# A recurrent first stage and its cross-attention, overlapped at the seam: the second stage's first unit between the first stage's last projection and its last output product, one subtraction moved to GpSimd, and the mean square read behind the scan

## The chip, the cores and the metric

The program runs on one core of a Trainium2 chip. The metric is the device time of one execution in microseconds (us). The core has five engines that each work through their own list of instructions in order: TensorE (PE; its weight loads are shown apart as PEld), VectorE (DVE), ScalarE (ACT), GpSimd (POOL) and SyncE (SP), which here only starts transfers. An engine waits for another by a counter (a semaphore).

## What is computed

The reference is a two-layer decoder on 16 sequences of 128 tokens with 256 channels, with a layer norm after each of its six sub-layers. The change touches the first two.

```
x = layernorm(x + hgrn(x))                 # stage A
x = layernorm(x + cross_attention(x, ctx)) # stage B
x = layernorm(x + top2_experts(x))         # stage C
...                                        # three more sub-layers
```

```
def hgrn(x):                       # stage A
    i, f, g = x @ Wi, x @ Wf, x @ Wg
    i = silu(i) * sigmoid(-f)
    a = sigmoid(f)
    o = scan over tokens: h = a * h + i
    o = o * rsqrt(mean(o*o) + eps) * gnorm * silu(g)
    return o @ Wo

def cross_attention(X, Z):         # stage B; X, Z are (channels, tokens) blocks
    q, k, v = Wq X + bq, Wk Z + bk, Wv Z + bv
    p = softmax(where(mask, k^T q, -inf) / sqrt(128))
    return v p
```

## The kernel before

The tokens are cut into NU = 8 units of two sequences (UB = 2, so 256 tokens a unit). Each stage is written out by hand, once for every engine, as a list of steps with lags: `pipelined(engine, NU, [(lag, step), ...])` calls, in turn s, each step of the list in its order for unit s - lag. Buffers are used by turns (`slot` is the unit's parity). Nothing is scheduled by a program: an engine runs what stands next in its list, and waits there.

Stage A, for a unit t:

- ACT `a_x_high` (L726) rounds the unit of X to its high part xp_hi; DVE `a_x_low` (L1101) subtracts that from X and writes the low part xp_lo (128x512). The three projections on PE, `a_proj` (L1606), are 36 matmuls that take products of high and low parts, and fill banks 0 to 5.
- ACT `a_gates` (L738 to L743) takes four sigmoids. DVE `a_scan` multiplies (L1121, L1126 from the banks; L1130, gb, from memory) and runs two scans (L1133), then multiplies the scan's result by the gate (L1140, og).
- ACT `a_square` (L753) squares the scan's result. PE `a_out` sums the squares with eight tiny matmuls (L1635) and makes the output product (L1640) in banks 7 and 6.
- DVE `a_msq` (L1147) reads the mean square; POOL `a_rms` (L610) takes its inverse root; DVE `a_sub` (L1157, y) adds the scaled product to X; the layer norm's statistics follow (L1077, L1081, and the variance L1083). POOL takes the root of the variance (L597) and makes the shift (L603, L606), and ACT `a_apply` (L758) writes the normalised rows back to X.

PE's `a_out` for a unit waits until the variance of the unit before is written, since bank 6 must have been read.

Stage B, for a unit: PE `b_proj` makes queries, keys and values (L1655, L1659, L1665, banks 0 to 2); ACT copies its context rows (`b_copy`, L772) and takes queries and values out of the banks (`b_evac`, L778 and L783), DVE the keys (`b_keys`, L1175); PE `b_scores` (L1676, L1677, banks 3 and 4); DVE takes the maximum (L1180), ACT the exponentials (`b_exp`, L792), DVE divides by the sum (L1184, L1189); PE transposes (`b_xpose`, L1688, banks 5 and 6) and makes the output (`b_out`, L1699, bank 7), and a layer norm follows (DVE L1196, L1077 to L1083, POOL L597, DVE L1090).

Between the two stages each engine first ends its list of stage A. DVE then waits for all rows of stage A to be normalised, makes the scaled bias and the mask (L1167, L1169), and only after these do ACT and PE begin stage B:

```
            pe.wait_ge(sem("B_consts"), 2)
            loaded(pe, "ld_b")
            pe.wait_ge(sem("ln_var"), LN["B"])
```

## Time and profile before

| | |
|---|---|
| median of three runs | 812.95 us (812.26 to 814.93) |
| the profiled execution | 808.24 us, of it 806.5 us from first to last instruction |
| PE busy | 704.8 us (87%) |
| DVE busy | 556.4 us (69%) |
| ACT busy | 469.1 us (58%) |
| POOL busy | 234.6 us (29%) |
| stage A, first projection to last variance | 7.7 to 84.7 us |
| stage B, first projection to last router product | 88.3 to 171.2 us |

The timeline view lists an engine's instructions in order of time; a row with xN merges N of them. The number in brackets at a row's end is how long the engine was idle before it, and what ended that wait. The view of windows gives, for a stretch of time, the busy time of each engine, then the clock that TensorE was granted (1.00 is the full 2.4 GHz, 0.50 is 1.2 GHz), then the share of the transfer engines and the rate in GB/s.

### The profile page before, as it was taken

How to read it: one execution, taken by the hardware profiler on the slowest of the kernel's cores; microseconds unless marked ns; L12 is line 12 of the kernel's file. 1: busy time of each engine (PE TensorE's matmuls, PEld its weight loads, DVE VectorE, ACT ScalarE, POOL GpSimd, SP SyncE). 2: the span in 40 equal slices, each digit the busy share in tenths (PEclk: the TensorE clock that was granted, in tenths of full speed). 3: DMA queues.
4: the chain of work that ended last, by engine and by line, in shares of the span. 5: the costliest groups of instructions: out<-in, count | busy, mean ns of one | idle time of the engine just before them, and what ended most of it. 6: DMA issues, size and time to landing. Idle time of an engine off the chain costs nothing.

```text
span 806.5 us, 17830 instructions
## 1 busy us (share of the span) xinstructions
PE 704.8 (87%) x5074; PEld 627.8 (78%) x5075; DVE 556.4 (69%) x1498; ACT 469.1 (58%) x1179; POOL 234.6 (29%) x399
## 2 busy tenths in 40 slices
PE   6887699958864988999999999999699989999972
PEld 5886477734432988999998999999599978888872
DVE  4786387757888446777786788887566765555376
ACT  4453466538782227777776788887345545555433
POOL 3122200033334600112121121111154515555544
PEclk9999699966695899999999999999699999999996
DMA  9940000000002586656667566652025433333162
GB/s 291 355 118 0 1 1 1 0 0 1 0 1 105 154 278 203 179 162 202 190 189 207 146 192 168 160 157 74 0 84 136 144 95 98 97 99 102 45 227 79
DMA packets 66486, 95.59 MB, mean 119 GB/s; under 512 B 11391, under 2 KB 52993, under 8 KB 66305
## 3 DMA queue, kind: packets, MB, share of 16 engines
q1 hardware_dynamic: 63024, 86.51, 36.3%
q0 software_dynamic: 3408, 8.43, 2.9%
q8 instruction: 26, 0.43, 0.2%
q14 instruction: 28, 0.22, 0.1%
HBM read 62.45 MB, written 33.36 MB: 119 GB/s over the span
## 4 chain that ended last, share of the span: by engine, by line
PE 58%; issue 16%; DVE 12%; DMA 4%; POOL 3%; ACT 3%; SPq 3%; DVEq 0%; POOLq 0%; ACTq 0%
PE bank L1875 13%; PE bank L1861 7%; PE bank L1951 6%; PE bank L2017 5%; PE bank L1850 4%; PE bank L1844 3%; PE bank L2041 3%; PE bank L1968 3%; PE bank L1606 3%; PE bank L1891 2%; PE bank L2005 2%; SPq L478 1%; DMA k_D<-stage_d 1%; DVE X L1090 1%; PE bank L1640 1%
## 5 line engine op out<-in xcount | busy, mean ns | idle before, releaser
L1875 PE MATMUL bank<-f_mem,late_mem 128*128 128x68 f32 (+3 forms) x1024 | 127.9, 268 | 0.0
L1875 PEld LDWEIGHTS bank<-f_mem,late_mem 128*128 128x128 f32 x1024 | 124.5, 192 | 0.7 <-issue 0.5
L597 POOL TENSOR_TENSOR rstd<-var,power 128x2 f32<-128x2 f32 (+1 forms) x64 | 41.7, 651 | 219.4 <-DVE var L1083 208.5
L1336 DVE TENSOR_REDUCE smax<-bank 128x4 f32<-128x512 f32 x128 | 88.2, 690 | 22.3 <-PE bank L1850 20.9
L915 ACT ACTIVATE late_mem<-bank 128x512 f32<-128x512 f32 x128 | 77.7, 607 | 21.6 <-PE bank L1861 19.3
L905 ACT ACTIVATE late_mem<-bank,smax 128x128 f32<-128x128 f32 x256 | 73.8, 384 | 11.4 <-DVE smax L1336 11.4
L1861 PE MATMUL bank<-ident,late_mem 128*128 128x128 f32 x512 | 77.3, 273 | 2.9 <-ACT late_mem L905 1.6
L1850 PE MATMUL bank<-kz,qs 128*128 128x256 f32 x256 | 75.1, 376 | 0.0
L1861 PEld LDWEIGHTS bank<-ident,late_mem 128*128 128x128 f32 x512 | 59.2, 141 | 3.6 <-ACT late_mem L905 2.0
L899 ACT ACTIVATE late_mem<-late_mem 128x512 f32<-128x512 f32 x64 | 41.0, 641 | 24.1 <-DVE late_mem L1343 23.3
L1850 PEld LDWEIGHTS bank<-kz,qs 128*128 128x128 f32 x256 | 48.7, 191 | 6.1 <-issue 0.3
L1951 PE MATMUL bank<-x_hi,w_hi 128*128 128x256 f32 x176 | 51.6, 293 | 1.0 <-DVE x_lo L1400 1.0
L1951 PE MATMUL bank<-x_lo,w_hi 128*128 128x256 f32 x176 | 50.8, 288 | 0.0
L1951 PE MATMUL bank<-x_hi,w_lo 128*128 128x256 f32 x176 | 50.7, 288 | 0.0
L1844 PE MATMUL bank<-causal,identb 128*128 128x512 bf16 x128 | 48.7, 381 | 1.2 <-DVE hidden_mem L1327 1.2
L1343 DVE TENSOR_TENSOR late_mem<-bank,smax 128x512 f32<-128x512 f32 x64 | 44.3, 692 | 6.9 <-DVE smax L1336 0.5
L686 POOL DMA_INDIRECT xg<-X,idx x32 | 33.6, 1049 | 42.7 <-DMA xg<-X,idx 21.2
L698 POOL DMA_INDIRECT yg<-attn_w,dest x39 | 38.8, 995 | 20.4 <-issue 12.0
L1968 PE MATMUL bank<-w_hi,hid_hi 128*128 128x256 f32 (+1 forms) x96 | 29.9, 311 | 13.8 <-DVE hid_lo L1417 13.7
L977 ACT ACTIVATE f_mem<-bank 128x256 f32<-128x256 f32 x40 | 15.3, 384 | 40.9 <-PE bank L1951 40.7
L1407 DVE TENSOR_TENSOR f_mem<-bank,f_mem 128x256 f32<-128x256 f32 x40 | 17.0, 424 | 30.0 <-ACT f_mem L977 29.7
L627 POOL TENSOR_TENSOR late_mem<-late_mem,f_mem 128x256 bf16<-128x256 bf16 x32 | 21.4, 669 | 52.1 <-DVE late_mem L1271 52.1
(285 smaller groups left out, 2069.9 us busy)
## 6 DMA issues: line engine op xcount, KB each, us to landing
qs<-q_D SPq DMA_DIRECT2D x64, 128.0 KB, 2.7
kz<-k_D SPq DMA_DIRECT2D x128, 64.0 KB, 2.6
qs<-q_E SPq DMA_DIRECT2D x64, 128.0 KB, 2.7
kz<-k_E SPq DMA_DIRECT2D x128, 64.0 KB, 2.5
xg<-f_mem SPq DMA_DIRECT2D x1, 5031.0 KB, 22.7
late_mem<-xg SPq DMA_DIRECT2D x39, 129.0 KB, 2.1
q_D<-stage_d SPq DMA_DIRECT2D x8, 512.0 KB, 2.9
k_D<-stage_d SPq DMA_DIRECT2D x8, 512.0 KB, 4.0
```

The lines of the kernel that those rows point to most:

```text
L597: gp.tensor_tensor(rstd[:, slot, 0:n], var[:, slot, 0:n], power[:, 0:n], ALU.pow).then_inc(sem("ln_rstd"), 1)
L899: sc.activation(sp[:, g, :, :], sp[:, g, :, :], ACT.Exp).then_inc(sem("core_exp"), 1)
L905: ins = sc.activation(sp[:, g, i, :], bank[g][:, i * P:(i + 1) * P], ACT.Exp, bias=smax[:, g, i:i + 1])
L915: sc.activation(spt[:, g, :, :], bank[4 + g % 2][:, :], ACT.Copy).then_inc(sem("core_pts"), 1)
L1336: ve.tensor_reduce(smax[:, g, :], v, axis=AX.X, op=ALU.max, negate=g not in SUBS).then_inc(sem("core_max"), 1)
L1343: ve.tensor_tensor(sp[:, g, :, :], v, smax[:, g, :].unsqueeze(2).to_broadcast([P, HG, P]), ALU.subtract).then_inc(sem("core_sub"), 1)
L1844: mm(bank[g][:, :], identb[:, :], causal[:, :].unsqueeze(1).to_broadcast([P, HG, P]), start=True, stop=False)
L1850: ins = mm(bank[g][:, i * D:(i + 1) * D], qs[slot][:, a_ * P:(a_ + 1) * P], kz[:, slot, :, a_ * P:(a_ + 1) * P], start=False, stop=(i == 1))
L1861: ins = nc.tensor.transpose(bank[4 + g % 2][:, i * P:(i + 1) * P], sp[:, g, i, :], ident[:, :])
L1875: ins = mm(bank[6][:, h * (DH + 1):to * (DH + 1)], spt[:, g, i, :], vf[:, slot, h:to, :].rearrange("p h d -> p (h d)"), start=True, stop=True)
L1951: ins = mm(bank[r][:, m * UT:(m + 1) * UT], w[:, lo:lo + P], x[:, t % 2, k, :], start=(n == 1), stop=(n == 3 * KC))
L1968: ins = mm(halves(6 + t % 2)[:, j, :], h[lanes, r, cols], v[lanes, w], start=(f == n == j == 0), stop=(f == NF - 1 and n == 2 and j == UB ...
```

## The change

Four things are changed; all other code is the same.

1. Low part of X: `a_x_low` moves from DVE's list to POOL's, at the head of each turn, for units 1 to 7. Unit 0's stays on DVE. On POOL the steps `a_rms`, root and shift have lag 2 instead of 1, which leaves their order among themselves as it was.
2. Mean square: DVE's `a_scan` is split. The multiplication og is now its own step `a_gated`, and `a_msq` stands between the scans and it.
3. PE's `a_out` waits for the two reads of bank 6 by `a_sub` (`ln_stats`) instead of for the variance.
4. Seam: `b_proj` and `b_scores` of unit 0 stand on PE between `a_proj` of unit 7 (and `a_out` of unit 6) and `a_out` of unit 7. ACT's and DVE's steps for that unit are put into the last turns of stage A: the bias and mask at the end of DVE's turn 7, the rest in turns 8 and 9. The exponentials of unit 0 stand on ACT between the `a_apply` of units 6 and 7, and their division on DVE between mean square and `a_sub` of unit 7. ACT loads one table with both exponential and logarithm ahead of them, and the load that stood ahead of stage C is gone. PE's transposes of unit 0 wait for the last variance of stage A.

```
+            def a_x_low(t, slot):
+                pool.wait_ge(sem("A_xh"), t + 1)
+                gp.tensor_tensor(xp_lo[:, slot, :, :], tokens(XT, t), xp_hi[:, slot, :, :], ALU.subtract
+                                 ).then_inc(sem("A_xl"), 1)
-            pipelined(pool, NU, [(1, a_rms), (1, inverse_root("A")), (1, a_shift)])
+            pipelined(pool, NU, [(0, but_first(a_x_low)), (2, a_rms), (2, inverse_root("A")), (2, a_shift)])
...
-            pipelined(act, NU, [(0, a_x_next), (1, a_gates), (1, a_square), (3, a_apply)])
...
-            pipelined(act, NU, [(0, b_copy), (1, b_evac), (2, b_pt), (4, c_xt), (1, b_exp)])
+            def exp_table():
+                sc.preload_act_table_set("natural_log_exp_and_others")
+            pipelined(act, NU, [(0, a_x_next), (1, only_at(NU - 1, (b_copy, (0, 0)))), (1, a_gates),
+                                (1, only_at(NU - 1, (b_evac, (0, 0)))), (1, a_square),
+                                (1, only_at(NU - 1, (b_evac_v, (0, 0)))), (3, but_last(a_apply)),
+                                (1, only_at(NU - 1, (b_copy, (1, 1)), (exp_table, ())))])
+            b_exp(0, 0)
+            a_apply(NU - 1, (NU - 1) % 2)
+            pipelined(act, NU, [(0, lambda t, slot: None if isinstance(t, int) and t < 2 else b_copy(t, slot)),
+                                (1, but_first(b_evac)), (1, but_first(b_evac_v)), (2, b_pt), (4, c_xt),
+                                (1, but_first(b_exp))])
...
-            pipelined(dve, NU, [(0, a_x_next), (1, a_scan), (2, a_msq), (2, stats)])
-            dve.wait_ge(sem("ln_x"), LN["B"])
...
-            pipelined(dve, NU, [(0, b_keys), (2, apply), (0, b_max), (2, c_copy), (3, c_scores), (1, stats)])
+            pipelined(dve, NU, [(1, a_scan), (2, a_msq), (2, only_at(NU - 1, (b_norm, (0, 0)))), (1, a_gated),
+                                (1, only_at(NU - 1, (b_keys, (0, 0)))), (2, a_stats),
+                                (1, only_at(NU - 1, (b_max, (0, 0)))), (1, only_at(NU - 2, (b_consts, ())))])
+            pipelined(dve, NU, [(0, but_first(b_keys)), (2, apply), (0, but_first(b_max)), (0, but_first(b_norm)),
+                                (2, c_copy), (3, c_scores), (1, stats)])
...
                 if not (isinstance(t, int) and t < 1):
-                    pe.wait_ge(sem("ln_var"), t)
+                    pe.wait_ge(sem("ln_stats"), 3 * UB * t - 2 * UB)
...
-            pipelined(pe, NU, [(0, a_proj), (1, a_out)])
-            pe.wait_ge(sem("B_consts"), 2)
-            pe.wait_ge(sem("ln_var"), LN["B"])
...
+            pipelined(pe, NU, [(0, a_proj), (1, only_at(NU - 1, (b_proj, (0, 0)), (b_scores, (0, 0)))), (1, a_out)])
+            pipelined(pe, NU, [(0, but_first(b_proj)), (1, b_xpose), (3, c_xpose), (0, but_first(b_scores)), (3, c_router),
+                               (1, b_out)])
```

How the lists stand now. First DVE, one turn of stage A, before (late turns stand outside the loop, in the loop's order; up_mem holds the gates and the scan, bank the projections; "waits" names the semaphores waited for):

```order
L1101 TENSOR_TENSOR xp_lo<-XT_mem,xp_hi 128x512 [waits A_xh]
L1121 TENSOR_TENSOR up_mem<-bank,up_mem 128x512 [waits A_gates]
L1124 MEMSET up_mem 128x4
L1126 TENSOR_TENSOR up_mem<-bank,up_mem 128x512
L1130 TENSOR_TENSOR up_mem<-up_mem 128x512 [waits A_si,A_hsq]
L1133 SCALAR_TENSOR_TENSOR up_mem<-up_mem 128x256 [waits A_own]
L1133 SCALAR_TENSOR_TENSOR up_mem<-up_mem 128x256
L1140 TENSOR_TENSOR up_mem<-up_mem 128x512 [waits A_h,A_si,A_o]
L1147 TENSOR_SCALAR msq<-bank 128x2 [waits A_o]
L1157 SCALAR_TENSOR_TENSOR y<-bank,rms,X 128x256 [waits ln_x,A_rms]
```

With the change:

```order
L1146 TENSOR_TENSOR up_mem<-bank,up_mem 128x512 [waits A_gates]
L1149 MEMSET up_mem 128x4
L1151 TENSOR_TENSOR up_mem<-bank,up_mem 128x512
L1155 TENSOR_TENSOR up_mem<-up_mem 128x512 [waits A_si,A_hsq]
L1158 SCALAR_TENSOR_TENSOR up_mem<-up_mem 128x256 [waits A_own]
L1158 SCALAR_TENSOR_TENSOR up_mem<-up_mem 128x256
L1174 TENSOR_SCALAR msq<-bank 128x2 [waits A_o]
L1167 TENSOR_TENSOR up_mem<-up_mem 128x512 [waits A_h,A_si,A_o]
L1184 SCALAR_TENSOR_TENSOR y<-bank,rms,X 128x256 [waits ln_x,A_rms]
```

The subtraction is gone from the head of DVE's turn, and the mean square (now L1174) stands ahead of og (now L1167). On POOL the subtraction heads the turn:

```order
L632 ISA [waits A_xh]
L632 TENSOR_TENSOR xp_lo<-XT_mem,xp_hi 128x512
L626 REGISTER_ALU
L627 TENSOR_TENSOR rms<-msq,power 128x2 [waits A_msq]
L614 TENSOR_TENSOR rstd<-var,power 128x2 [waits ln_var]
L620 TENSOR_TENSOR nmean<-mv,minus 128x2
L623 TENSOR_TENSOR nbias<-nmean,rstd 128x2 [waits ln_rstd,A_minus]
```

It stands behind the shift of the turn before, that is behind the variance of the unit three before. PE at the seam, before (behind unit 7's projection and unit 6's output product):

```order
L1635 MATMUL bank<-ones,up_mem 128x1 [waits ln_var,A_hsq]
L1635 MATMUL bank<-ones,up_mem 128x1 x3
L1640 MATMUL bank<-late_mem,up_mem 128x256 [waits A_og]
L1640 MATMUL bank<-late_mem,up_mem 128x256 x3
L1655 MATMUL bank<-X,hidden_mem 128x512 [waits ln_var,ld_b,ln_x,B_consts,consts]
L1659 MATMUL bank<-f_mem,hidden_mem 128x512 [waits B_xs]
```

and with the change:

```order
L1684 MATMUL bank<-X,hidden_mem 128x512 [waits A_gates,A_si,ld_b,ln_x]
L1688 MATMUL bank<-f_mem,hidden_mem 128x512 [waits B_xs]
L1694 MATMUL bank<-hidden_mem,f_mem 128x128 x4
L1709 MATMUL bank<-maskb,identb 128x256 [waits B_consts,consts,A_si,B_ks,B_qs]
L1710 MATMUL bank<-late_mem 128x256
```

```order
L1668 MATMUL bank<-ones,up_mem 128x1 [waits ln_stats,A_hsq]
L1668 MATMUL bank<-ones,up_mem 128x1 x3
L1673 MATMUL bank<-late_mem,up_mem 128x256 [waits A_og]
L1673 MATMUL bank<-late_mem,up_mem 128x256 x3
L1684 MATMUL bank<-X,hidden_mem 128x512 [waits B_qs,ln_x]
L1688 MATMUL bank<-f_mem,hidden_mem 128x512 [waits B_ks,B_xs]
L1694 MATMUL bank<-hidden_mem,f_mem 128x128 [waits B_vs]
L1694 MATMUL bank<-hidden_mem,f_mem 128x128 x3
L1724 MATMUL bank<-ident,late_mem 128x128 [waits B_p,ln_var,A_si]
```

Unit 0's projection and scores (L1684 to L1710) are ahead of unit 7's output product (L1668, L1673) now; unit 1's projection follows it at once, and the first wait for the end of stage A is at the transposes (L1724). ACT in the same place, with the change:

```order
L781 ACTIVATE X<-y,nbias,rstd 128x256 [waits A_shift]
L781 ACTIVATE X<-y,nbias,rstd 128x256
L814 ACTIVATE late_mem,psum_row<-bank,nmax 128x256 [waits B_max]
L814 ACTIVATE late_mem,psum_row<-bank,nmax 128x256
L814 ACTIVATE late_mem,psum_row<-bank,nmax 128x256 [waits B_max]
L814 ACTIVATE late_mem,psum_row<-bank,nmax 128x256
L781 ACTIVATE X<-y,nbias,rstd 128x256 [waits A_shift]
L781 ACTIVATE X<-y,nbias,rstd 128x256
L790 ACTIVATE f_mem<-ctx_mem 128x512 [waits B_proj]
L798 ACTIVATE late_mem<-bank,bqs 128x512 [waits B_q]
```

The queries of unit 1 leave their bank (L798) only behind unit 7's `a_apply` (the second L781 pair), which waits for the last shift of stage A.

## Rows read from the trace of the kernel before

**Rows 1.** Windows: stretch, busy us (instructions) by engine, PE clock, DMA share, GB/s
```profile
28.50:32.70 4.20, 4.16 (x16) 3.62 (x17) 3.98 (x8) 0.30 (x1) 1.02 (x3) 0.59 1.08 369
88.20:93.80 5.60, 5.54 (x14) 3.44 (x15) 0.75 (x1) 1.89 (x4) 0.85 (x1) 0.50 0.01 3
95.90:164.00 68.10, 65.06 (x381) 51.45 (x379) 51.54 (x161) 43.00 (x114) 5.46 (x8) 1.00 0.00 1
```
**Rows 2.** Timeline of DVE, stage A: start us, us, what [idle before]
```profile
36.19 0.17 DVE L1083 TENSOR_SCALAR var<-mv 128x2 f32<-128x2 f32 x1
...
54.13 0.68 DVE L1121 TENSOR_TENSOR up_mem<-bank,up_mem 128x512 f32<-128x512 f32 x1
...
56.06 1.27 DVE L1133 TENSOR_TENSOR_SCAN up_mem<-up_mem 128x256 f32<-128x256 f32 x2
57.46 0.69 DVE L1140 TENSOR_TENSOR up_mem<-up_mem 128x512 f32<-128x512 f32 x1
...
59.15 0.87 DVE L1157 SCALAR_TENSOR_TENSOR y<-bank,rms,X 128x256 f32<-128x256 f32 x2 [0.93 <-POOL rms L610]
...
61.13 0.17 DVE L1083 TENSOR_SCALAR var<-mv 128x2 f32<-128x2 f32 x1
61.32 0.69 DVE L1101 TENSOR_TENSOR xp_lo<-XT_mem,xp_hi 128x512 fp32r<-128x512 f32 x1
61.93 0.68 DVE L1121 TENSOR_TENSOR up_mem<-bank,up_mem 128x512 f32<-128x512 f32 x1
```
**Rows 3.** Timeline of PE: a turn of stage A, the seam, unit 1 of stage B
```profile
32.72 0.47 PE L1606 MATMUL bank<-xp_hi,wa_hi 128*128 128x256 f32 x1
...
37.22 0.95 PE L1635 MATMUL bank<-ones,up_mem 128*128 128x1 f32 x8
38.03 1.97 PE L1640 MATMUL bank<-late_mem,up_mem 128*128 128x256 f32 x8
...
76.48 1.46 PE L1635 MATMUL bank<-ones,up_mem 128*128 128x1 f32 x8 [4.50 <-DVE var L1083]
...
88.26 2.04 PE L1655 MATMUL bank<-X,hidden_mem 128*128 128x512 f32 x2 [6.70 <-DVE maskb L1169]
...
99.47 0.27 PE L1676 MATMUL bank<-maskb,identb 128*128 128x256 bf16 x1
...
101.64 1.89 PE L1699 MATMUL bank<-late_mem 128*128 128x256 f32 x8
```
**Rows 4.** Timeline of POOL: stage A, and a subtraction of the same shape
```profile
58.30 0.69 POOL L610 TENSOR_TENSOR rms<-msq,power 128x2 f32<-128x2 f32 x1 [3.10 <-DVE msq L1147]
61.38 1.18 POOL L597 TENSOR_TENSOR rstd<-var,power 128x2 f32<-128x2 f32 x1 [2.38 <-DVE var L1083]
...
62.79 0.20 POOL L606 TENSOR_TENSOR nbias<-nmean,rstd 128x2 f32<-128x2 f32 x1
...
164.71 1.26 POOL L636 TENSOR_TENSOR wd_lo<-attn_w,wd_hi 128x512 fp32r<-128x512 f32 x1
```
**Rows 5.** Timeline of POOL, near the end
```profile
790.75 1.21 POOL L708 TENSOR_TENSOR X<-X,late_mem 128x512 f32<-128x512 f32 x1
```
**Rows 6.** Timeline of DVE, the same stretch
```profile
790.83 1.68 DVE L1567 TENSOR_TENSOR ctx_mem<-ctx_mem,late_mem 128x512 f32<-128x512 f32 x1
```
**Rows 7.** Timeline of ACT, the seam and unit 0 and 1 of stage B
```profile
85.95 1.09 ACT L758 ACTIVATE X<-y,nbias,rstd 128x256 f32<-128x256 f32 x2 [7.29 <-POOL nbias L606]
...
94.37 1.28 ACT L792 ACT_TABLE_LOAD   x1
95.75 0.47 ACT L792 ACTIVATE late_mem<-bank,nmax 128x256 f32<-128x256 f32 x1
...
97.75 0.62 ACT L772 ACTIVATE f_mem<-ctx_mem 128x512 f32<-128x512 f32 x1
```
**Rows 8.** Timeline of DVE, the mask, and half of the division of unit 0
```profile
87.15 1.01 DVE L1169 TENSOR_SCALAR maskb<-mask 128x512 bf16<-128x512 uint8 x1
...
98.09 0.62 DVE L1189 TENSOR_SCALAR late_mem<-late_mem,rrow 128x256 f32<-128x256 f32 x2
```

More of the change, by code:

```diff
@@ L120, in pipelined_pair, with but_first, other, only_at @@
         turn(s)
+def but_first(step):
+    def other(t, slot):
+        if not (isinstance(t, int) and t == 0):
+            step(t, slot)
+    return other
+def only_at(turn, *steps):
+    def other(t, slot):
+        if isinstance(t, int) and t == turn:
+            for step, args in steps:
+                step(*args)
+    return other
 RING = 3
@@ L809, in c_xt, with but_last, other @@
                 sc.activation(tokens(XTB, t), halves(2), ACT.Copy).then_inc(sem("C_xt"), 1)
-            pipelined(act, NU, [(0, b_copy), (1, b_evac), (2, b_pt), (4, c_xt), (1, b_exp)])
+            def but_last(step):
+                def other(t, slot):
+                    if not (isinstance(t, int) and t == NU - 1):
+                        step(t, slot)
+                return other
+            def exp_table():
[9 more added lines that the diff above has]
+                                (1, but_first(b_exp))])
             def route_exp():
@@ L852, in _ @@
             route_exp()
-            def but_first(step):
-                def other(t, slot):
-                    if not (isinstance(t, int) and t == 0):
-                        step(t, slot)
-                return other
             def c_round(t, slot):
@@ L1107, in _ @@
                 if k == 0:
-                    a_x_low(0, 0)
-            def a_x_next(t, slot):
-                if not (isinstance(t, int) and t < 1):
-                    a_x_low(t, slot)
+                    dve.wait_ge(sem("A_xh"), 1)
+                    ve.tensor_tensor(xp_lo[:, 0, :, :], tokens(XT, 0), xp_hi[:, 0, :, :], ALU.subtract
+                                     ).then_inc(sem("A_wl"), 1)
             loaded(dve, "ld_a2")
@@ L1135, in a_scan, with a_gated @@
                 ins.then_inc(sem("A_h"), 1)
+            def a_gated(t, slot):
                 if not (isinstance(t, int) and t < 2):
@@ L1194, in b_sub @@
                 dve.wait_ge(sem("B_o"), t + 1)
+                if isinstance(t, int) and t < 1:
+                    dve.wait_ge(sem("ln_x"), LN["B"])
                 for j in range(UB):
@@ L1612, in a_proj @@
             def a_proj(t, slot):
-                pe.wait_ge(sem("A_xl"), t + 1)
+                if not (isinstance(t, int) and t < 1):
+                    pe.wait_ge(sem("A_xl"), t)
                 if not (isinstance(t, int) and t < 2):
@@ L1654, in b_proj @@
                     pe.wait_ge(sem("B_qs"), t)
+                else:
+                    loaded(pe, "ld_b")
+                    pe.wait_ge(sem("A_gates"), 4 * NU - 2)
+                    pe.wait_ge(sem("A_si"), 2 * NU - 3)
                 mm(halves(0), xq[:, :], xrows(t), start=True, stop=True).then_inc(sem("B_q"), 1)
@@ L1670, in b_scores @@
                 pe.wait_ge(sem("B_ks"), t + 1)
+                if isinstance(t, int) and t < 1:
+                    pe.wait_ge(sem("consts"), CONSTS)
+                    pe.wait_ge(sem("B_consts"), 2)
+                    pe.wait_ge(sem("A_si"), 2 * NU - 1)
                 for j in range(UB):
@@ L1681, in b_xpose @@
             def b_xpose(t, slot):
+                if isinstance(t, int) and t < 1:
+                    pe.wait_ge(sem("A_si"), 2 * NU)
+                    pe.wait_ge(sem("ln_var"), LN["B"])
                 for j in range(UB):
```

27 lines of the change are left out of this document (12 added, 15 removed).

## The prediction
> **What bounds the kernel now.** I read the slices of the page first: TensorE is 87% busy over the span, with two thin places early on, and the change touches only the first 165 us. So I asked three things. What sets the turn of stage A? What lies empty at the seam? And is stage B, behind it, bound by PE, so that a start earlier by so much ends earlier by as much?
>
> The turn of stage A: from unit 5's first multiplication at 54.13 to unit 6's at 61.93 is 7.80 us [rows 2]. DVE does nothing else but work through its list, and stands idle 0.93 us once, ahead of y, for POOL's root. PE's turn at full clock takes 4.50 us of projection (32.72 to 37.22) and 2.78 us of sums and output product, whose end overlaps the next projection: 7.3 us at most, I take 7.0 [rows 3]. So DVE bounds stage A, and PE is 0.8 us behind.
>
> The seam: PE waits 4.50 us for the variance ahead of unit 7's sums, and 6.70 us for the mask ahead of stage B [rows 3], and after the second wait it runs at a granted clock of 0.50 (1.2 GHz) for 5.6 us [rows 1].
>
> Stage B: from 95.9 to 164.0 us PE is busy 65.1 of 68.1 us at clock 1.00 [rows 1], while DVE and ACT are busy 52 and 43. PE bounds it from unit 1 on. I measure the gain at one point therefore: the start of unit 1's scores, 99.47 us before [rows 3]. What is earlier there is earlier at the end.
>
> **The turn of stage A.** Edit 1 takes 0.61 us (61.32 to 61.93) [rows 2] from DVE's turn and edit 2 lays og's 0.61 over POOL's root. If nothing else happened, DVE's turn would be 7.80 - 0.61 - 0.6 = 6.6 us and PE would bound.
>
> Two rows say that it will not be so. DVE's multiplication of two SBUF operands took 1.68 us at 790.83, against 0.69 for one of that shape at 57.46 [rows 6, 2]; POOL's addition of the same shape had begun 0.08 us earlier and lasted till 791.96 [rows 5], and DVE ended 0.55 behind it. The other way round, POOL's root at 61.38, begun 0.06 behind DVE's subtraction, took 1.18 instead of 0.69 and ended 0.55 behind that [rows 4, 2]. So these pairs do not overlap: the later waits out the earlier. The Trainium skill (SBUF — State Buffer, Who interferes with whom) says this of every Vector instruction with two SBUF inputs beside a GpSimd one that reads SBUF, which speaks against both moves of stage A; by that rule the trace agrees, and it leaves y free, whose one operand is a bank.
>
> Now I follow one turn from V, the end of a variance. POOL's root starts 0.08 later and takes 0.69 (nothing blocks it now), the shift ends 0.43 behind it (62.56 to 62.99) [rows 4]: V + 1.2. The subtraction starts at V + 1.3 and takes 1.26, the duration of the one of that shape and type at 164.71 [rows 4]: V + 2.56. DVE wants gb (two SBUF inputs) about 1.2 us behind the start of its turn, so inside this stretch; it ends at V + 3.11. Scans to the start of og: 1.40 (56.06 to 57.46) [rows 2], so V + 4.55. og ends at V + 5.24. The root of the mean square starts about 0.05 behind og (the mean square itself ends as the scans do), is blocked, and ends at V + 5.79; y starts 0.16 later (58.99 to 59.15), and the next variance ends 2.15 behind that (59.15 to 61.30) [rows 2]: 8.10 us a turn, against 7.80.
>
> PE does not shorten that: unit 1's variance ended at 36.36 [rows 2]; with mean square earlier and the first collisions I put it at 36.0. Four turns give 68.4, and the bias and mask on DVE, now between turns 7 and 8, 1.1 (1.01 for the mask [rows 8]): unit 7's first multiplication starts at 69.5. Stage A gains nothing. The bounds of a turn are 7.3 (no collision; PE's limit) and 8.5 (the subtraction itself blocked, at the 1.68 us of a blocked instruction [rows 6]).
>
> **The seam.** From 69.5, in order:
> - og ends 4.0 later (54.13 to 58.15) [rows 2], the keys behind it 0.7 (a 128x512 instruction, [rows 2]): 74.3. PE has made unit 0's projection meanwhile; ACT has copied and evacuated in its idle time.
> - Scores of unit 0: 2.2 (99.47 to 101.64) [rows 3]: 76.5. Sums and output product of unit 7: 2.8 [rows 3]: 79.3. This is the removed wait of 4.50, now filled.
> - On ACT, the table load (1.28) [rows 7] is over before unit 6's shift comes: y of unit 6 starts at 74.3, variance 76.4, shift 77.6. Apply takes 1.0 [rows 7], the four exponentials 2.0 (95.75 to 97.75) [rows 7]: 80.6. **This is a new wait**: the division of unit 0 stands on DVE ahead of y of unit 7, and ends 0.8 behind the exponentials [rows 8], 81.4, though POOL's root of unit 7 was ready at about 80.2.
> - y and variance of unit 7, 2.15: 83.6. PE's transposes of unit 0 can start. The shift is there at 84.8.
> - On ACT apply of unit 7 (1.0), the copy for unit 2 and the queries of unit 1 (two 128x512 instructions of 0.6) [rows 7] follow one another: 87.0. Scores of unit 1 start at 87.1.
>
> The Trainium skill (ScalarE: Activation LUTs, What ACT_TABLE_LOAD costs) gives about 2.66 us for a switch with its drain; here 94.37 to 95.75 [rows 7] shows 1.38 to the next instruction, so the row decides. By the page's figure apply of unit 6 would start 0.5 later and the sum would be 0.5 higher.
>
> 99.47 - 87.1 = **12.4 us earlier**. Against this: PE has work for only 1 us (the transposes) between unit 1's projection, which ends at about 81.9, and 87.1. Twice in these stages the clock was down with PE busy: 28.5 to 32.7 at 0.59, a loss of 4.2 x 0.41 = 1.7 us, and 88.2 to 93.8 at 0.50, a loss of 2.8 us [rows 1]. Unit 1's scores and unit 0's output product should lie in such a stretch now, behind the point at which I measure. Nothing is the lower bound; the second row has a long gap in front, as here, so I take **2.8**. The second table load that goes was not waited for, and stage C starts as before. Edit 3 (the wait for the reads) only starts products that then wait for a projection: nothing.
>
> Sum: 12.4 - 2.8 = 9.6 us less. On the profiled execution's 808.24 that is 798.6; it lies 4.7 below the median of the runs, 812.95, from which I take the same 9.6: **803.4 us**.
>
> **Rivals.**
> - The collisions cost less: POOL's root may come before og and then be free of it (8.1 - 0.55 = 7.55 a turn), or the subtraction finds DVE busy with instructions that do not collide (PE's 7.3). Four turns give 2.2 to 3.2 more, in the middle 800.7. For it: 0.05 us is a thin margin. Against it: two rows show full blocking.
> - The clock stays up: PE stands still 1.7 us, works 1.0, and stands still 2.5, no single gap as long as the 4.50 and 6.70 of before. Then the 2.8 us are not lost: 800.6; with the case above 797.9.
> - The collisions cost more, or the in-order waits of the two interleaved stages add up: 8.5 a turn is 1.6, and each of ACT and DVE could be a step late, another 2: 807.0.
> - No difference: stage A's list on DVE turns out so much slower that it eats the seam; that takes turns of over 10 us.
> - **Slower:** in stage A PE now stands still about 8.1 - 7.0 = 1.1 us a turn or more, before 0.8. If that makes its clock fall and stay down, a turn takes twice PE's 7.0, 14 instead of 8.1 us. Two such turns take 11.8 us and more than the gain; all five make 29.5, so 812.95 - 9.6 + 29.5 = 832.8. It decides where a gap outlasts what the clock forgives, which lies above the 0.8 of before and at or below the 4.50 of the seam. Against it: a turn longer by 0.3 us changes little.
>
> **How the numbers follow.** The forecast gets 0.50; more gain (fewer collisions, the clock kept, or both) 0.32; dearer collisions 0.10; no difference 0.04; slower 0.04. The predicted time is that of the likeliest, 803.4. The range takes in both gains nearly whole and the dearer case: 798.0 to 808.0. A measurement of this kernel tells 0.3% (2.4 us) from no change. Faster by that: 0.50 + 0.32 + 0.10 = 0.92, within it 0.04, slower 0.04.
>
> **What would show it.** In DVE's timeline gb (L1155) at 1.2 to 1.5 us instead of 0.68, and POOL's L627 at about 1.2 instead of 0.69, say that the pairs collide; turns of 8.1. PE's unit 7 sums directly behind scores with no idle; DVE's y of unit 7 behind the division of unit 0 and not behind POOL; PE's scores of unit 1 released by ACT's queries, at 87, in a window at clock 0.5 to 0.6. From there to the end every distance as before. I am wrong if the gain does not stand at the scores of unit 1, if stage A's turn leaves 7.3 to 8.5, or if PE is idle inside stage B from unit 2 on.

## The result, and the profile after

| | before | with the change |
|---|---|---|
| median | 813.25 us (812.26 to 814.93) | 802.84 us, three executions (798.12 to 802.98) |
| ratio, 95% interval | | 0.9851 (0.9804 to 0.9898) |
| profiled execution, and its span | 808.24 us, 806.5 us | 802.98 us, 801.2 us |
| PE / DVE / ACT / POOL busy | 704.8 / 556.4 / 469.1 / 234.6 us | 706.2 / 556.6 / 466.9 / 244.9 us |

The forecast was 803.4 us. The changed kernel was run twice more, as the control of the experiments; the ratio was 0.9865 both times. The medians fell by 10.4, 11.9 and 12.0 us. The ratio is not the quotient of the two medians (that is 0.987 here and 0.985 in both controls), so the two readings of a total differ by up to 0.2%. A fourth execution of the changed kernel took 1689.29 us and is left out here and in the ratio; with it the median would be 802.91 us.

First a turn of stage A, the one that [rows 2] show of before. The timeline of DVE, changed kernel; columns as there:

```profile
53.53 0.69 DVE L1146 TENSOR_TENSOR up_mem<-bank,up_mem 128x512 f32<-128x512 f32 x1 [0.55 <-ACT up_mem L766]
...
54.75 1.24 DVE L1155 TENSOR_TENSOR up_mem<-up_mem 128x512 f32<-128x512 f32 x1
56.02 1.27 DVE L1158 TENSOR_TENSOR_SCAN up_mem<-up_mem 128x256 f32<-128x256 f32 x2
57.21 0.14 DVE L1174 TENSOR_SCALAR msq<-bank 128x2 f32<-128x2 f32 x1
57.33 0.69 DVE L1167 TENSOR_TENSOR up_mem<-up_mem 128x512 f32<-128x512 f32 x1
58.72 0.88 DVE L1184 SCALAR_TENSOR_TENSOR y<-bank,rms,X 128x256 f32<-128x256 f32 x2 [0.70 <-POOL rms L627]
...
60.70 0.17 DVE L1115 TENSOR_SCALAR var<-mv 128x2 f32<-128x2 f32 x1
61.43 0.69 DVE L1146 TENSOR_TENSOR up_mem<-bank,up_mem 128x512 f32<-128x512 f32 x1 [0.56 <-ACT up_mem L766]
```

The timeline of POOL in the same turn:

```profile
53.06 0.69 POOL L614 TENSOR_TENSOR rstd<-var,power 128x2 f32<-128x2 f32 x1 [2.40 <-DVE var L1115]
...
54.17 1.27 POOL L632 TENSOR_TENSOR xp_lo<-XT_mem,xp_hi 128x512 fp32r<-128x512 f32 x1
57.42 1.14 POOL L627 TENSOR_TENSOR rms<-msq,power 128x2 f32<-128x2 f32 x1 [1.99 <-DVE msq L1174]
```

The turn is 7.90 us (53.53 to 61.43), against 7.80. Both collisions are there. gb (L1155) began inside POOL's subtraction, took 1.24 us instead of 0.68, and ended 0.55 behind it (54.17 + 1.27 = 55.44; 54.75 + 1.24 = 55.99). The root of the mean square began 0.09 behind og, took 1.14 and ended 0.54 behind it, where before it took 0.69 [rows 4]. And DVE now waits 0.55 us at the head of its turn for ACT's gates, since PE waits for the same subtraction: in PE's timeline the idle of 0.71 below. The work that left DVE came back as waits. From variance to variance, units 1 to 5, the turns are 7.89, 8.26, 7.89 and 7.86 us; before they were 8.86, 8.26, 7.82 and 7.68.

So one turn, unit 2's, did get shorter, and for another reason. PE ahead of unit 1's sums, in the kernel before and in the changed one:

```profile
28.54 1.32 PE L1635 MATMUL bank<-ones,up_mem 128*128 128x1 f32 x8 [2.54 <-DVE var L1083]
```

```profile
27.55 1.05 PE L1668 MATMUL bank<-ones,up_mem 128*128 128x1 f32 x8 [0.81 <-DVE y L1184]
```

Before, PE waited 2.54 us for the variance, and the granted clock behind that wait was 0.59 from 28.5 to 32.7 [rows 1]. With edit 3 it waits 0.81 us, for y's read of the bank, and the clock stays at 1.00. Of the 13 profiles of kernels with edit 3, the controls and the experiments included, 12 have unit 2's turn at 7.1 to 7.9 us; the exception is told below. No run has edit 3 alone, so that it is the cause is argued and not shown.

Then the seam, the timeline of PE:

```profile
55.67 0.38 PE L1638 MATMUL bank<-xp_hi,wa_hi 128*128 128x256 f32 x1 [0.71 <-POOL xp_lo L632]
...
74.10 0.27 PE L1709 MATMUL bank<-maskb,identb 128*128 128x256 bf16 x1 [0.77 <-issue]
...
76.27 0.95 PE L1668 MATMUL bank<-ones,up_mem 128*128 128x1 f32 x8
...
83.23 1.06 PE L1724 MATMUL bank<-ident,late_mem 128*128 128x128 f32 x8 [1.57 <-issue]
86.60 0.39 PE L1709 MATMUL bank<-maskb,identb 128*128 128x256 bf16 x1 [2.30 <-ACT late_mem L798]
...
90.84 2.34 PE L1735 MATMUL bank<-late_mem 128*128 128x256 f32 x8
93.01 1.02 PE L1684 MATMUL bank<-X,hidden_mem 128*128 128x512 f32 x2
```

The waits of 4.50 and 6.70 us [rows 3] are gone. Unit 7's sums (76.27) follow unit 0's scores directly. What is left are 0.77, 1.57 and 2.30 us. The first two have no releaser in the view ("issue"): the first ends 0.11 us behind the keys of unit 0 (DVE's L1198, 73.25 to 73.99), the second 0.10 behind the variance of unit 7 (83.13), for which the transposes wait. The last is for the queries of unit 1. These start at 86.60, against 99.47 [rows 3]. The timelines of DVE and ACT say why they were not there sooner:

```profile
68.70 0.42 DVE L1192 TENSOR_SCALAR maskb<-mask 128x512 bf16<-128x512 uint8 x1
69.31 0.69 DVE L1146 TENSOR_TENSOR up_mem<-bank,up_mem 128x512 f32<-128x512 f32 x1 [0.19 <-ACT up_mem L766]
...
80.98 0.87 DVE L1184 SCALAR_TENSOR_TENSOR y<-bank,rms,X 128x256 f32<-128x256 f32 x2
...
82.96 0.17 DVE L1115 TENSOR_SCALAR var<-mv 128x2 f32<-128x2 f32 x1
```

```profile
75.49 1.28 ACT L840 ACT_TABLE_LOAD   x1
77.31 1.09 ACT L781 ACTIVATE X<-y,nbias,rstd 128x256 f32<-128x256 f32 x2 [0.54 <-POOL nbias L623]
...
84.36 1.09 ACT L781 ACTIVATE X<-y,nbias,rstd 128x256 f32<-128x256 f32 x2 [4.15 <-POOL nbias L623]
85.36 0.61 ACT L790 ACTIVATE f_mem<-ctx_mem 128x512 f32<-128x512 f32 x1
85.88 0.67 ACT L798 ACTIVATE late_mem<-bank,bqs 128x512 f32<-128x512 f32 x1
```

ACT stands 4.15 us ahead of unit 7's apply, and the queries of unit 1 (L798), whose bank PE had filled by about 80, are queued behind it. Last, the clock, by windows (columns as in [rows 1]):

```profile
84.00:85.00 1.00, 0.29 (x3) 0.05 (x1) 0.00 (x0) 0.64 (x2) 0.92 (x3) 0.95 0.00 0
85.00:86.00 1.00, 0.00 (x0) 0.00 (x0) 0.00 (x0) 1.00 (x3) 1.00 (x2) 0.50 0.00 0
...
91.00:92.00 1.00, 1.00 (x5) 0.80 (x4) 0.88 (x3) 0.19 (x1) 0.00 (x0) 0.63 0.00 0
```

The granted clock is 0.50 from 85 to about 91.5 (before it was 0.50 from 77 to 94). The scores of unit 1 and the output of unit 0 took 6.41 us together (86.60 to 93.01), against 3.90 before (99.47 to 103.37).

### The profile page after: what moved, and what is told of

It reads as the page before. It is cut to its first block, busy times and chain, and to the rows that moved or that the text cites. A ratio compares the mean times of both kernels' runs of the same rounds, so it can differ in the third digit from the quotient of the medians.

```text
span 801.2 us, 17829 instructions
## 1 busy us (share of the span) xinstructions
PE 706.2 (88%) x5074; PEld 628.8 (78%) x5075; DVE 556.6 (69%) x1491; ACT 466.9 (58%) x1178; POOL 244.9 (31%) x406
## 4 chain that ended last, share of the span: by engine, by line
PE 56%; issue 15%; DVE 14%; ACT 5%; DMA 3%; POOL 3%; SPq 2%; DVEq 0%; POOLq 0%; ACTq 0%
PE bank L1913 13%; PE bank L1899 7%; PE bank L2055 5%; PE bank L1989 5%; PE bank L1638 4%; PE bank L1888 4%; PE bank L1882 3%; PE bank L2079 3%; PE bank L2006 3%; PE bank L1929 2%; PE bank L2043 2%; SPq L495 1%; POOL rstd L614 1%; DVE X L1122 1%; PE bank L1805 1%
## 5 line engine op out<-in xcount | busy, mean ns | idle before, releaser
L721 POOL DMA_INDIRECT yg<-attn_w,dest x39 | 38.8, 994 | 20.7 <-issue 12.6
L2006 PE MATMUL bank<-w_hi,hid_hi 128*128 128x256 f32 (+1 forms) x96 | 30.4, 317 | 14.6 <-DVE hid_lo L1449 14.3
L1638 PE MATMUL bank<-xp_hi,wa_hi 128*128 128x256 f32 x96 | 29.0, 302 | 12.4 <-DVE xp_lo L1135 8.1
```

What stands on the lines that cost most here:

```text
L1638: ins = mm(out, a_, b_, start=(n == 1), stop=(n == 3 * len(terms)))
L2006: ins = mm(halves(6 + t % 2)[:, j, :], h[lanes, r, cols], v[lanes, w], start=(f == n == j == 0), stop=(f == NF - 1 and n == 2 and j == UB ...
```

## How far one profile carries

The changed kernel's profile is 10.8 us ahead of the one before at unit 0's variance in stage B (95.57 against 106.33), and only 5.3 us at the end: it lost 5.5 us in code that, but for a table load, the edit does not touch. The two controls tell what that is.

> The changed kernel once more, with nothing edited, to have it on the same chip as the three runs below and to see how far executions of one and the same program lie apart. Expected: a median within 1.5 us of 802.9, a ratio to the kernel before of 0.987 (0.984 to 0.990), unit 7's first multiplication within 0.3 us of 69.3 and the scores of unit 1 within 0.3 us of 86.6. If single executions of one program spread by up to 5 us, as the 798.1 beside 802.8 and 803.0 suggests, the offset between the two traces behind the seam cannot be read from one profile of each; if they don't, the 4 to 5 us that the traces lose between stage C and the end are an effect of the change.

Measured: 801.3 us (795.72 to 802.56), ratio 0.9865 (0.9842 to 0.9889). Unit 7's first multiplication was at 68.63 and the scores of unit 1 at 85.92, both 0.7 us earlier than expected.

> The change as it is, on the same chip as the three others of this group. Expected: ratio 0.984 to 0.989 as in its first two measurements, unit 7's first multiplication within 0.8 us of 69.3, seven steady turns as before; its profile once more shows where executions of one program differ: the start (loads, up to 0.8 us), the low clock of the seam (0 to 2.5 us), and low-clock stretches between 160 and 460 us.

Measured: 800.28 us (798.01 to 803.75), ratio 0.9865 (0.9827 to 0.9903). Here the two places are 67.94 (outside the expected 0.8 us) and 85.23. Both differences were there at the start. DVE's second multiplication of unit 0, in the kernel before and in the profile above:

```profile
15.43 0.68 DVE L1126 TENSOR_TENSOR up_mem<-bank,up_mem 128x512 f32<-128x512 f32 x1
```

```profile
16.18 0.68 DVE L1151 TENSOR_TENSOR up_mem<-bank,up_mem 128x512 f32<-128x512 f32 x1
```

In the controls it is at 15.45 and 14.82. Counted from it, the scores of unit 1 start at 84.04 before and at 70.42, 70.47 and 70.41 in the three profiles of the change: 13.6 us earlier each time.

What lies behind the seam is less steady. Two variances in the timeline of DVE, the first control:

```profile
128.03 0.17 DVE L1115 TENSOR_SCALAR var<-mv 128x2 f32<-128x2 f32 x1
...
315.34 0.15 DVE L1115 TENSOR_SCALAR var<-mv 128x1 f32<-128x1 f32 x1
```

and the second:

```profile
127.51 0.17 DVE L1115 TENSOR_SCALAR var<-mv 128x2 f32<-128x2 f32 x1
...
318.80 0.15 DVE L1115 TENSOR_SCALAR var<-mv 128x1 f32<-128x1 f32 x1
```

The same instructions of the same program took 187.3 us in one execution and 191.3 in the other. Of the 4.0 us, 2.7 arise before 245 us, in a stretch with many low-clock pieces: from 150 to 260 us the granted clock changes between 0.50 and 1.00 several times, and where it does so differs from profile to profile. The first control is 12.6 us ahead of before at stage B's first variance and 12.5 at the last one of all; for the second control it is 12.8 and 10.2, for the profile shown above 10.8 and 5.3. So from here on a place is read in the profile, and a total from the ratio and the medians alone.

## The experiments

**The seam alone.** Stage A's edits 1 and 2 are undone; edit 3 stays. The part on DVE (the subtraction's step goes back from POOL's list to DVE's too):

```
-            pipelined(dve, NU, [(1, a_scan), (2, a_msq), (2, only_at(NU - 1, (b_norm, (0, 0)))), (1, a_gated),
+            pipelined(dve, NU, [(0, but_first(a_x_low)), (1, a_scan), (1, a_gated), (2, a_msq), (2, only_at(NU - 1, (b_norm, (0, 0)))),
```

> The seam alone: stage A's two edits are undone (the low parts back on VectorE at the head of its turn, the mean square behind the gated product), the moved first unit of stage B stays. Theory (the seam carries the gain, stage A's edits are a wash): steady turns of 7.80 us, unit 7's first multiplication at 69.3, the gated product of VectorE's unit 7 ahead of the mean square of unit 6, which puts y of unit 6 and the keys of unit 0 about 0.7 us later, scores of unit 1 at 86.6 to 87.3; median 0 to 1 us above the control. Rival (stage A's edits carry part of the gain): unit 7's first multiplication at 71 or later and a median 2 us or more above the control.

Measured: 800.1 us, ratio 0.9855 (0.9831 to 0.9879); turns of 7.83 and 7.80 us, scores of unit 1 at 86.59. The theory holds: with the seam and edit 3 there, edits 1 and 2 bring nothing. Unit 2's turn is 7.81 us here too, against 8.86 before, so that shorter turn is not theirs.

**Stage A's edits alone**, in the kernel before. Edit 3 is among them:

```
-            pipelined(dve, NU, [(0, a_x_next), (1, a_scan), (2, a_msq), (2, stats)])
+            pipelined(dve, NU, [(1, a_scan), (2, a_msq), (1, a_gated), (2, stats)])
-            pipelined(pool, NU, [(1, a_rms), (1, inverse_root("A")), (1, a_shift)])
+            pipelined(pool, NU, [(0, but_first(a_x_low)), (2, a_rms), (2, inverse_root("A")), (2, a_shift)])
...
-                    pe.wait_ge(sem("ln_var"), t)
+                    pe.wait_ge(sem("ln_stats"), 3 * UB * t - 2 * UB)
```

> The kernel before with stage A's two edits alone (low parts on GpSimd, mean square ahead of the gated product, the output product waiting for bn_stats in place of the variance), the seam as before. Theory: the collisions take back what the edits give; steady turns of 7.9 us, unit 7's first multiplication at 69.3, stage B's start as before; 812 to 814, that is within 1 us of the kernel before. Rival: the edits gain by themselves and the seam needs less; turns of 7.4 and 809 or lower.

Measured: 809.54 us, ratio 0.9946 (0.9924 to 0.9968). Both were wrong: a gain of about 4 us (3.6 by the medians, 4.4 by the ratio), and yet turns of 7.9. The timeline of PE, this kernel:

```profile
73.42 1.84 PE L1648 MATMUL bank<-ones,up_mem 128*128 128x1 f32 x8 [3.70 <-DVE y L1169]
...
85.59 2.04 PE L1668 MATMUL bank<-X,hidden_mem 128*128 128x512 f32 x2 [6.70 <-DVE maskb L1181]
```

The steady turns gain nothing, but the last two do. From unit 5's variance to unit 7's it is 14.3 us here (67.55 to 81.87) and 15.7 before (68.81 to 84.55), as the last turn is a bare chain, in which an earlier mean square counts, and as PE, by edit 3, no longer waits for the variance (3.70 against 4.50 us [rows 3]). Another 1.0 us is unit 2's turn, 8.86 us before and 7.90 here, with the granted clock at 1.00 where before had 0.59. With the seam, unit 0's projection and scores fill that wait of PE, and the last two turns are as long with edits 1 and 2 as without (14.4 us in either profile): what they bring there alone, the seam has already taken.

**One edit undone each.** The low parts back on VectorE, at the head of its turn:

> The changed kernel with one part undone: the low parts of X back on VectorE at the head of its turn, the mean square still ahead of the gated product. Theory (it is the shared port of VectorE and GpSimd that takes the gain of stage A: gb took 1.2 to 1.6 us beside the subtraction, 0.68 without): gb at 0.68, the gate product of unit s+1 behind a subtraction of 0.69, turns of 7.4 us; unit 7's first multiplication at 66.6 to 67.5 and a median 2 to 3 us below the control. Rival (VectorE's own work bounds the turn, so moving 0.7 us back costs it): turns of 8.3 or more and a median 2 us above the control. If the root of the mean square still takes 1.2 us here, it is the gated product beside it, not the subtraction, that slows it.

Measured: 794.45 us, ratio 0.9796 (0.9761 to 0.9831), outside the interval of the control: a gain over the change as it is. The timeline of DVE, this kernel:

```profile
50.76 0.69 DVE L1140 TENSOR_TENSOR xp_lo<-XT_mem,xp_hi 128x512 fp32r<-128x512 f32 x1
...
52.58 0.68 DVE L1155 TENSOR_TENSOR up_mem<-up_mem 128x512 f32<-128x512 f32 x1
...
58.09 0.17 DVE L1109 TENSOR_SCALAR var<-mv 128x2 f32<-128x2 f32 x1
```

gb is 0.68 again and the turn 7.54 us (variances at 50.55 and 58.09). The root of the mean square still took 1.25, so it is og that blocks that one. What the profile shows in place is 2.0 us at stage B's first variance (91.71 against 93.73 in the first control), of which 0.5 was there at unit 0's first multiplication. The forecast was a median 2 to 3 us lower; the medians differ by 6.9. The rest is not shown in any place, and by the section above executions of one program differ by as much.

The mean square back behind og, the low parts left on GpSimd:

> The fourth corner of stage A's two edits, with the seam kept: low parts on GpSimd, mean square back behind the gated product. Measured so far are both undone (800.1 us, turns of 7.8), low parts on VectorE with the mean square ahead (794.5, turns of 7.54), and both as changed (801.3, turns of 7.9). Theory (the two edits are independent terms: mean square ahead saves about 0.3 us a turn, the subtraction on GpSimd costs about 0.35): turns of 8.1 to 8.3 us and 803 to 805. Rival (the mean square ahead only helps where the low parts are on VectorE, since its root then runs beside the gated product and the two cancel): turns of 7.9 and 801.

Measured: 805.11 us, ratio 0.989 (0.9855 to 0.9926), turns of 8.2. A turn of the four combinations: 7.80 (both undone), 7.54 (mean square ahead), 8.2 (low parts on GpSimd), 7.9 (both). The edits are two independent terms, -0.3 and +0.4 us. This is also the one profile with edit 3 in which the clock fell in stage A: 0.50 from 29.5 to 36, behind a wait of PE of 1.10 us, and unit 2's turn took 9.07; the change as it is waited 0.81 and 1.65 us there and kept the clock. So 0.9 us of this profile (9.07 against 8.2) is not the collision's price. Here gb met the subtraction earlier in its course and waited longer, and again ended 0.55 behind it (POOL's row first):

```profile
55.68 1.26 POOL L632 TENSOR_TENSOR xp_lo<-XT_mem,xp_hi 128x512 fp32r<-128x512 f32 x1
```

```profile
55.96 1.53 DVE L1155 TENSOR_TENSOR up_mem<-up_mem 128x512 f32<-128x512 f32 x1
```

**The low parts at another place of GpSimd's turn**, between the two roots:

```
-            pipelined(pool, NU, [(0, but_first(a_x_low)), (2, a_rms), (2, inverse_root("A")), (2, a_shift)])
+            pipelined(pool, NU, [(3, a_rms), (0, but_first(a_x_low)), (3, inverse_root("A")), (3, a_shift)])
```

> The changed kernel with the low parts still on GpSimd, but one place later in its turn: between the root of the mean square and the root of the variance, so that they run beside y and bn_stats of VectorE in place of gb and the scans. Theory (what costs in stage A is that the subtraction meets gb and the scans on the shared port): gb back at 0.68 us, the two scans at 1.27, turns of 7.4 to 7.6 us, and a ratio to the kernel before of 0.980 like the run with the low parts on VectorE (794.5 us there). Rival (the subtraction costs the turn wherever it meets VectorE, or the root behind it comes late): turns of 7.9 or more, ratio 0.986 or above.

Measured: 796.4 us, ratio 0.9797 (0.9765 to 0.983), turns of 7.35 us. Timelines of POOL and of DVE, this kernel:

```profile
41.25 1.26 POOL L632 TENSOR_TENSOR xp_lo<-XT_mem,xp_hi 128x512 fp32r<-128x512 f32 x1 [1.08 <-ACT xp_hi L749]
```

```profile
41.24 0.75 DVE L1109 BATCH_NORM_STATS2 st<-y 128x6 f32<-128x256 f32 x2
...
44.26 0.68 DVE L1155 TENSOR_TENSOR up_mem<-up_mem 128x512 f32<-128x512 f32 x1
```

The same subtraction, on the same engine, now lies beside bn_stats (0.75, as everywhere) and neither takes longer; PE has no wait over 0.2 us between 28 and 69 us any more. The root of the mean square still takes 1.14 beside og. This settles the cause in stage A: not the load of an engine, but which instruction of the other lies beside it. The Trainium skill (SBUF — State Buffer, Who interferes with whom) has it that a Vector instruction with at most one SBUF input, outside the modes that use two ports, does not contend with GpSimd; the trace agrees, with 0.75 for bn_stats beside the subtraction and without it.

**The queries first** on ScalarE:

```
-            a_apply(NU - 1, (NU - 1) % 2)
...
-                                (1, but_first(b_evac)), (1, but_first(b_evac_v)), (2, b_pt), (4, c_xt),
+                                (1, but_first(b_evac)), (1, but_first(b_evac_v)), (1, only_at(1, (a_apply, (NU - 1, (NU - 1) % 2)))), (2, b_pt), (4, c_xt),
```

> The changed kernel with one move on ScalarE: the application of stage A's last unit stands behind the evacuation of unit 1's queries and values, not ahead of it. Theory (the scores of unit 1 started late, 2.3 us of TensorE idle, because ScalarE stood 4.15 us waiting for unit 7's nbias with the queries behind it): that idle goes down to the wait for the keys, some 0.3 us; scores of unit 1 begin 4.4 us behind the end of the values' product instead of 4.9 - that is 84.2 instead of 86.6 on the clock of the control's shape, and the shorter pause may save some of the low clock too: ratio 0.9865 less 0.003 to 0.006. Rival (the scores wait for something else of the same time, keys or the freed bank, or the saved time is given back at unit 0's output): ratio unchanged and another releaser on the idle.

Measured: 797.32 us, ratio 0.9788 (0.9743 to 0.9833). The timeline of PE, this kernel:

```profile
83.03 1.06 PE L1723 MATMUL bank<-ident,late_mem 128*128 128x128 f32 x8 [1.57 <-issue]
83.93 0.27 PE L1708 MATMUL bank<-maskb,identb 128*128 128x256 bf16 x1
...
87.83 1.02 PE L1683 MATMUL bank<-X,hidden_mem 128*128 128x512 f32 x2
```

The scores of unit 1 stand directly behind the transposes, and they and the output of unit 0 take 3.90 us (83.93 to 87.83), with the granted clock at 1.00 in every window from 66 to 102 us. The wait of 2.30 was the queries' place in a list, and without it the clock did not fall, though the wait of 1.57 is still there. All seven profiles that keep the 2.30 us wait (the change, its controls and four experiments) have a stretch of 0.50 behind it. At stage B's first variance this profile is 2.9 us ahead of the first control's, although its stage A ran 0.5 us later. The ratio is lower than the 0.9805 to 0.9835 that was expected; its interval takes in nearly all of that.

**Filling the pauses** with matmuls whose results nobody reads (n1 = 12 and n2 = 16, then 12 and 20):

```
+            def keep_warm(sem_name, count, b, n):
+                pe.wait_ge(sem(sem_name), count)
+                for k in range(n):
+                    mm(halves(b)[:, k & 1, :], identb[:, :], maskb[:, k & 1, :], start=True, stop=True)
-            pipelined(pe, NU, [(0, but_first(b_proj)), (1, b_xpose), (3, c_xpose), (0, but_first(b_scores)), (3, c_router),
+            pipelined(pe, NU, [(0, but_first(b_proj)), (0, only_at(1, (keep_warm, ("A_si", 2 * NU, 5, n1)))), (1, b_xpose),
+                               (0, only_at(1, (keep_warm, ("A_msq", NU, 7, n2)))),
+                               (3, c_xpose), (0, but_first(b_scores)), (3, c_router),
```

> The changed kernel with 12 matmuls (128x256, bf16, results never read) on TensorE in the pause ahead of the transposes of unit 0, and 16 in the pause ahead of the scores of unit 1. Theory (the low clock of 85 to 91 us follows the pauses of 1.6 and 2.3 us): the granted clock stays at 1.00 through the scores of unit 1 and the output of unit 0, which then take 2.17 and 1.73 us in place of 4.24 and 2.17 in the slowest profile, and the whole gains 1 to 2.5 us: ratio 0.984 to 0.986. Rival (the clock falls for what came before, the waits of stage A's end and the light load of the seam, or falls a little later instead): the low stretch stays or moves behind, and nothing is gained.

Measured: 803.94 us, ratio 0.9882 (0.9847 to 0.9917). The timeline of PE, with 12 and 16:

```profile
80.61 1.47 PE L1765 MATMUL bank<-maskb,identb 128*128 128x256 bf16 x12
82.34 1.06 PE L1724 MATMUL bank<-ident,late_mem 128*128 128x128 f32 x8 [0.26 <-issue]
83.24 1.91 PE L1765 MATMUL bank<-maskb,identb 128*128 128x256 bf16 x16
85.72 0.28 PE L1709 MATMUL bank<-maskb,identb 128*128 128x256 bf16 x1 [0.56 <-ACT late_mem L798]
```

The clock stayed at 1.00, the scores and the output took 3.91 us (85.72 to 89.63), and the profile was ahead of the control at stage B. So the low clock does follow the pauses. But the expected gain did not come: the median is 2.6 us above the control's, and the intervals of the two ratios overlap. The place where this profile loses is the loop of the routed experts 600 us later: from the last variance ahead of it to the first behind it, 214.2 us against 206.7 in the first control. The window of 680 to 730 us in the first control, and under it in this kernel:

```profile
680.00:730.00 50.00, 47.18 (x320) 42.04 (x319) 27.06 (x100) 25.96 (x80) 27.59 (x61) 1.00 0.34 102
```

```profile
680.00:730.00 50.00, 46.38 (x303) 40.16 (x304) 25.49 (x96) 24.93 (x76) 26.80 (x59) 1.00 0.32 96
```

Every other kernel did 319 or 320 matmuls there, at the same clock. The fill with 32 instead of 28 was made to ask whether the loop's place in PE's program matters:

> The fill of the pauses once more, with 12 and 20 dummy matmuls in place of 12 and 16. In the run with 28 the granted clock stayed at 1.00 through the seam, as its theory had it, and yet the time rose by 2.6 us: TensorE did 303 matmuls between 680 and 730 us where every other kernel did 319 or 320, in the routed experts' loop, which the edit does not touch. Theory (it is where the loop lies in TensorE's program: 28 matmuls with their weight loads are 56 more instructions ahead of it, and 32 make it 64, a round number): 319 or 320 matmuls in 50 us again and a ratio 0.984 to 0.986. Rival (dummy matmuls as such, or the data they read, slow the loop; or 64 is no better a shift than 56): 303 to 310 matmuls, ratio 0.988 or above.

Measured: 797.72 us, ratio 0.9813 (0.9772 to 0.9855), and in the window:

```profile
680.00:730.00 50.00, 47.33 (x320) 42.14 (x319) 26.95 (x100) 26.22 (x80) 27.73 (x60) 1.00 0.34 100
```

320 again, with more dummy matmuls than before, and 207.9 us for the stretch of the loop. So it is not the dummies as such. That it goes with how many instructions stand ahead of the loop fits both fills, but rests on one profile of each and is not shown. Why 56 more should cost 5% of the matmuls in 50 us and 64 nothing is open. The Trainium skill (Runtime: NRT & Kernel Launch, Instruction fetch mechanics) names a stall where the target of a taken branch is not in the two pages that are held and must be fetched first; the bytes on the instruction queues are 0.43 and 0.22 MB in both fills and in the control, so no run here shows an additional fetch.

**Both corrections together**, the queries first and the low parts on VectorE, and then with the low parts between GpSimd's two roots:

> Two corrections together: the low parts back on VectorE (mean square still ahead of the gated product), and stage A's last application behind the queries and values of unit 1 on ScalarE. Theory (they are terms of separate places, stage A's turn and the seam, and add up: 0.9796 and 0.9788 by themselves against 0.9865 for the change as it is): turns of 7.54 us, unit 7's first multiplication at 66.9, scores of unit 1 at 81.6 with TensorE at the full clock through the seam, ratio 0.972 to 0.977, 791 to 794. Rival (both mostly changed the share of executions that keep the full clock later on, and that is to be had once): ratio 0.978 or above.

Measured: 794.24 us (793.67 to 795.08), ratio 0.9783 (0.9748 to 0.9817): the rival's ratio. In place the terms do add up: stage B's first variance is at 88.07, 5.7 us ahead of the first control. But the profile then loses 4.7 us of its lead over the one before by the last variance (18.3 to 13.6), part of it right behind 140 us: the granted clock is 0.70 from 140 to 144, and the step between two variances there (139.63 to 145.99) takes 6.4 us, against 5.2 before. The total by itself cannot say whether this is worth more than either part.

> The same with the low parts on GpSimd between the two roots in place of VectorE. Theory: turns of 7.35 us as in the run that had this alone, unit 7's first multiplication at 65.8, scores of unit 1 at 80.5, and a ratio of 0.970 to 0.976, 1 us below the run with VectorE; below it if that 1 us is all. Rival: no better than the move of the low parts alone, 0.980.

Measured: 790.88 us (788.92 to 792.5), ratio 0.9744 (0.9708 to 0.9779), as forecast, with turns of 7.35 and the scores of unit 1 at 80.22. It is 3.4 us below the run with VectorE by the medians, where 1 was forecast, but the intervals of the two overlap. Its interval lies below that of the change as it is in all three measurements: 21 us under the kernel before, where the change is 10 to 12 under it.

## Why the prediction was right

The total was within a microsecond, and inside the range in the controls too. The nearness is in part luck: the forecast gain was 9.6 us, and the three measurements have 10.4, 11.9 and 12.0. The mechanism is the one forecast; what was short is named below. By its own steps:

- **The point of measurement.** "Scores of unit 1 at 87.1", 12.4 us earlier: 86.60, 12.9 earlier, or 13.6 when both are counted from unit 0. Each step of the chain was 0.3 to 0.5 early and in its order: end of the exponentials 80.2 (forecast 80.6), end of the division 81.07 (81.4), variance of unit 7 83.1 (83.6), its shift 84.3 (84.8). The new wait it named, y of unit 7 behind the division of unit 0, is there: 80.98, with no idle for POOL ahead of it.
- **The turn.** Forecast 8.10 for each of four, measured 7.89, 8.26, 7.89 and 7.86: 31.9 us instead of 32.4. Mechanism right, both collisions with the sizes told; the sum had 0.1 too much ahead of the subtraction (it began 1.19 behind the variance's end, not 1.3) and 0.1 between gb and og.
- **Unit 7's first multiplication**, forecast 69.5, was at 69.31 by errors that cancel. Unit 1's variance ended at 36.83 instead of 36.0, of which 0.75 was there at unit 0's multiplications; in the first control, which starts as before did, it ended at 36.11. The subtraction met the scans there, which took 2.22 instead of 1.27 us, and the turn was 8.06 against 7.96 before. The mask took 0.42 instead of 1.01: POOL was busy all the time beside the row of before [rows 8]; that it blocked the mask there is argued, not shown.
- **"Edit 3 ... nothing", and "stage A gains nothing".** This is where the sum was short. From unit 0's multiplications to unit 7's, stage A took 0.7 us less than before in the profile of the change and in both controls; the forecast had 0.2 more (69.5 against 69.28). The sum took 7.80 us as the turn of before and looked for the price of the collisions only. But unit 2's turn had been 8.86, behind PE's wait for the variance and the low clock that followed, and with edit 3, which shortens that wait, it was 7.89 (that edit 3 is the cause is argued, as no run has it alone). Edits 1 and 2 gain nothing, as forecast. By the collisions found in the rows of before, the subtraction could have been put where nothing collides, which is 0.5 us a turn. The rival "collisions cost less", at 7.3 to 7.55 us a turn, was not what the change does; it is what two of the experiments do, at 7.35 and 7.54.
- **The clock.** Forecast 2.8 lost behind the point of measurement, measured 2.5 in this profile and 1.7 in both controls. It is the other mis-sized term: the clock does fall behind a pause of 1.6 and one of 2.3 us, as the forecast took it and its rival did not, but the time at 1.2 GHz varies from one execution to the next. "Twice in these stages the clock was down with PE busy" leaves out a third time: unit 7's sums and output product before took 1.46 [rows 3] and 3.76 us from 76.48, against 0.95 and 1.97 at full clock. The sum does not use it.
- **"From there to the end every distance as before."** Wrong as a test: stretches of the same code differ by 4 us between two executions, so that sentence could not have been checked with one profile. The lead at stage B's first variance held to the end in the first control (12.6 and 12.5), and not in the other two profiles. The sign "PE is idle inside stage B from unit 2 on" did not show: from 93 to 145 us no wait of PE is over 0.3 us.
- The **slower** case did not come: PE's pauses in stage A were 0.7 to 1.65 us and the granted clock was 1.00 from 18 to 80 us. It was not far off, though: the experiment with the mean square behind og had the low clock there for one turn.

## What to carry to other kernels

Before work is moved from one engine to another, look at what will lie beside it: a two-operand subtraction on GpSimd cost 0.4 us a turn beside VectorE's own two-operand work, and nothing beside bn_stats. Once a seam is closed, look for the engine that waits longest in it and what is queued behind: one apply in front of the queries held PE for 2.3 us and cost the clock on top. A wait of PE that an edit shortens is not worth nothing because something else is waited for next: where it went from 2.54 to 0.81 us, the clock behind it stayed up and the turn was 1.0 us shorter. And where executions of one program lie 5 to 7 us apart, read a place from the profile and a total from medians, and never explain a total by one profile.

## What was not expected of the hardware

- A blocked gb, or a blocked root on GpSimd, ends 0.54 to 0.55 us behind the instruction that blocks it, wherever the two met (gb began 0.58 us into the subtraction and took 1.24; 0.28 into it, 1.53). How far behind is not the same for all: in the kernel before, POOL's short nmean (L603, 0.20 alone) at 45.95 took 0.49 beside DVE's subtraction and ended 0.05 behind it.
- The low clock of the seam began and ended at other times in executions of one program: the same scores and output took 6.41 us in one profile and 5.60 in two others, against 3.90 at full clock.
- With 28 matmuls put far ahead of a loop, one profile had 303 matmuls in 50 us of the loop, against 319 or 320 in all others, with 32 as well. The cause is open.
